# A routed expert stage: residual rows kept in sorted order instead of gathered by row number, and a single-tile ending

## What is computed

```python
logits = hidden @ router_w.T                      # 16 experts, the best one is taken (K = 1)
scores = sigmoid(top value)                       # 0 for the other 15 experts
routed_in = hidden * score
gate, up = split(routed_in @ gate_up_proj[e])     # 256 -> 2 x 256
routed_out = (up * silu(gate)) @ down_proj[e]     # 256 -> 256
shared = silu(hidden @ shared_gate_w.T) * (hidden @ shared_up_w.T) @ shared_down_w.T
x = layernorm(x + shared + routed_out)
```

## Time and profile before

| | |
|---|---|
| Median of three runs | 963.65 us |
| The profiled execution | 962.75 us |
| Its span, first to last instruction | 960.5 us |
| TensorE busy | 910.0 us, 95% |
| VectorE busy | 554.3 us, 58% |
| ScalarE busy | 351.4 us, 37% |
| GpSimd busy | 592.2 us, 62% |
| `route_and_share` begins | 680.5 us |
| `experts` begins | 844.1 us |

### The profile page before, as it was taken

The page is one execution under the profiler, slowest core; times in us unless marked ns, Lnnn a source line. Parts: engine busy times, 40 slices in busy tenths (PEclk is TensorE's granted clock), DMA queues, the critical chain, the costliest instruction groups (busy, mean ns, idle before and its releaser), DMA issues. The chain is left out here.

```text
span 960.5 us, 13006 instructions
## 1 busy us (share of the span) xinstructions
PE 910.0 (95%) x4616; PEld 537.4 (56%) x4616; DVE 554.3 (58%) x1123; ACT 351.4 (37%) x493; POOL 592.2 (62%) x397
## 2 busy tenths in 40 slices
PE   6998799999999999999999999999799999989993
PEld 2655354555565455555555465545578888855552
DVE  2897556667647667657667647644645121136562
ACT  2245244434335444425444425443341111124332
POOL 0453198888877888868888868893104400038885
PEclk9999899999999999999999999999799999999997
DMA  8013200000001000001000001040597100423310
GB/s 269 27 49 116 99 1 1 23 1 1 1 1 44 23 1 2 1 1 45 23 1 1 1 1 45 1 154 1 140 324 254 50 22 22 124 78 111 92 38 16
DMA packets 42873, 52.85 MB, mean 55 GB/s; under 512 B 4400, under 2 KB 33856, under 8 KB 42816
## 3 DMA queue, kind: packets, MB, share of 16 engines
q1 hardware_dynamic: 35808, 44.21, 14.7%
q0 software_dynamic: 3744, 6.32, 2.1%
q10 hardware_dynamic: 3264, 1.57, 0.6%
HBM read 38.42 MB, written 17.59 MB: 58 GB/s over the span
## 5 line engine op out<-in xcount | busy, mean ns | idle before, releaser
L600 POOL TENSOR_TENSOR accG<-accG,probs 128x1024 f32<-128x1024 f32 (+1 forms) x170 | 404.0, 2377 | 52.0 <-ACT probs L623 30.1
L623 ACT ACTIVATE probs<-st 128x1024 f32<-128x1024 f32 (+1 forms) x208 | 211.3, 1026 | 207.1 <-PE st L784 195.4
L667 DVE TENSOR_REDUCE mxp<-mx 128x1 f32<-128x512 f32 x360 | 231.6, 686 | 85.2 <-PE mx L770 79.0
L806 PE MATMUL av<-probs,V 128*64 128x512 f32 (+1 forms) x832 | 188.4, 596 | 0.0
L770 PE MATMUL mx<-K_hi,Q_hi 64*128 64x512 f32 (+1 forms) x480 | 164.0, 391 | 6.0 <-DVE mxp L667 4.5
L806 PEld LDWEIGHTS av<-probs,V 128*64 128x64 f32 (+1 forms) x832 | 56.8, 137 | 106.1 <-issue 100.6
L770 PEld LDWEIGHTS mx<-K_hi,Q_hi 64*128 64x128 f32 x480 | 78.9, 184 | 66.4 <-DVE mxp L667 34.5
L784 PE MATMUL st<-Q_hi,K_hi 64*128 64x512 f32 (+1 forms) x416 | 109.1, 440 | 0.9 <-ACT probs L623 0.9
L784 PE MATMUL st<-M,ones_r 64*128 64x512 f32 (+1 forms) x416 | 108.0, 394 | 0.0
L784 PE MATMUL st<-Q_hi,K_lo 64*128 64x512 f32 (+1 forms) x416 | 102.5, 391 | 0.0
L784 PE MATMUL st<-Q_lo,K_hi 64*128 64x512 f32 (+1 forms) x416 | 102.0, 390 | 0.0
(11 more groups left out here) (198 smaller groups left out, 1196.5 us busy)
## 6 DMA issues: line engine op xcount, KB each, us to landing
w_gate_up<-in_gate_up SPq DMA_DIRECT2D x4, 2048.0 KB, 20.8
w_down<-in_down SPq DMA_DIRECT2D x2, 2048.0 KB, 15.9
xs<-scratch_sorted_x SPq DMA_DIRECT2D x31, 128.5 KB, 2.1
scratch_sorted_x<-zero SPq DMA_DIRECT2D x7, 514.0 KB, 8.6
xT<-in_xT SPq DMA_DIRECT2D x4, 512.0 KB, 6.6
xring<-in_x SPq DMA_DIRECT2D x4, 512.0 KB, 9.4
scratch_x1b<-xT SPq DMA_DIRECT2D x4, 512.0 KB, 2.9
x<-scratch_x1b SPq DMA_DIRECT2D x4, 512.0 KB, 3.9
```

Source lines behind the costliest of these rows:

```text
L600: pool.tensor_tensor(total[0:r], so_far[0:r], probs[0:r, place(S, t)], ALU.add).then_inc(g_add, 1)
L623: act.activation(probs[0:r, place(S, t)], st[g % 2][0:r, :], ACT.Exp, scale=DH ** -0.5).then_inc(a_probs, 1)
L667: dve.tensor_reduce(mxp[:, F % 2, h * QT + i, j:j + 1], mx[h][:, 0:kn], AX.X, ALU.max).then_inc(v_mx, 1)
L806: mm = pe.matmul(av[h * DH:(h + 1) * DH, :], V[0:r, t, (2 * p + h) * DH:(2 * p + h + 1) * DH], probs[0:r, place(S, t), h * QC:(h + 1) * QC ...
```

## The change

- `routed` and its four `store_base` go. A new DRAM buffer `sorted_base` (31 tiles of 128 rows, 256 values) holds the base rows in sorted order. SP fills it with zeros from the tile `zero`, eight DMAs behind the last expert weight load of the gate and up part.
- In `route_and_share` POOL scatters `x2` tiles 0 to 11 into `sorted_base` by `pos`, 12 indirect DMAs behind its other 16, each after its tile's `v_base`, the first after the zero fill has landed (`d_bzero`).
- In `experts` POOL scatters tiles 12 to 15 first; the memory set of `base` and all 31 gathers go. SP waits for all 16 scatters, loads base tiles 0 to 3 with plain DMAs, and from then on takes turns: `xs` tile j, base tile j-4.
- The last three tiles (28, 29, 30, `SINGLE = 28`) have `inverse`, `shift` and the wait in `normalise` singly; POOL's stores stand between the inverses.

```diff
@@ route_and_share, sync
-            for c in range(CHUNKS - 1):
-                store_base(c)
+            for t in range(0, ETILES, ZT):
+                n = min(ZT, ETILES - t)
+                sp.dma_start(mem["sorted_base"].rearrange("(t p) n -> p t n", p=P)[:, t:t + n, :],
+                             zero[:, 0:D].unsqueeze(1).to_broadcast([P, n, D])
+                             ).then_inc(d_bzero, 16)
...
-            store_base(CHUNKS - 1)
@@ route_and_share, gpsimd
+            pool.wait_ge(d_bzero, 16 * ((ETILES + ZT - 1) // ZT))
+            for t in range(TILES - QT):
+                pool.wait_ge(v_base, t + 1)
+                pool.indirect_dma_start(mem["sorted_base"][:, :], bass.IndirectOffsetOnAxis(pos[:, t:t + 1], 0),
+                                        x2[:, t], None).then_inc(mem["d_base"], 16)
@@ experts, sync
             def load(j, r):
                 sp.wait_ge(p_x, j - UNROLL + 1)
                 sp.wait_ge(v_row, j - UNROLL + 1)
+                sp.sem_inc(filler, 1)
+                sp.dma_start(xs[:, r], xs_rows[:, bass.ds(j, 1), :].squeeze(1)).then_inc(d_xs[r], 16)
+            def load_base(j, r):
+                if not (isinstance(j, int) and j < AHEAD):
+                    sp.wait_ge(v_y, j - AHEAD + 1)
+                    sp.sem_inc(filler, 1)
+                sp.dma_start(base[:, r], base_rows[:, bass.ds(j, 1), :].squeeze(1)).then_inc(d_b[r], 16)
...
+            sp.wait_ge(mem["d_base"], 16 * TILES)
+            for j in range(AHEAD):
+                load_base(j, j)
+            for n in range(UNROLL):
+                turn(UNROLL + n, n)
@@ experts, gpsimd
-            pool.memset(base[:, :, :], 0.0).then_inc(g_c4, 1)
-            pool.wait_ge(g_c4, 3)
-            pool.wait_ge(mem["d_base"], 16 * CHUNKS)
-            def gather(j, r, reused):
...
+            for tile in range(TILES - QT, TILES):
+                pool.indirect_dma_start(mem["sorted_base"][:, :], bass.IndirectOffsetOnAxis(pos[:, tile:tile + 1], 0),
+                                        x2[:, tile], None).then_inc(mem["d_base"], 16)
...
-                if not (isinstance(j, int) and j + 2 >= ETILES):
-                    gather(j + 2, (n + 2) % UNROLL, not (isinstance(j, int) and j + 2 < AHEAD))
...
-            store(ETILES - 3, (ETILES - 3) % UNROLL)
-            store(ETILES - 2, (ETILES - 2) % UNROLL)
-            inverse(ETILES // 2, (ETILES - 1) % UNROLL, 1)
-            store(ETILES - 1, (ETILES - 1) % UNROLL)
+            inverse(single(SINGLE), SINGLE, SINGLE % UNROLL, 1)
+            store(SINGLE - 3, (SINGLE - 3) % UNROLL)
+            store(SINGLE - 2, (SINGLE - 2) % UNROLL)
+            inverse(single(SINGLE + 1), SINGLE + 1, (SINGLE + 1) % UNROLL, 1)
+            store(SINGLE - 1, (SINGLE - 1) % UNROLL)
+            store(SINGLE, SINGLE % UNROLL)
+            inverse(single(SINGLE + 2), SINGLE + 2, (SINGLE + 2) % UNROLL, 1)
+            store(SINGLE + 1, (SINGLE + 1) % UNROLL)
+            store(SINGLE + 2, (SINGLE + 2) % UNROLL)
@@ experts, vector
+                if isinstance(j, int) and j == SINGLE + 2:
+                    shift(single(SINGLE), SINGLE % UNROLL, 1)
+                elif n % 2 == 0 and not (isinstance(j, int) and (j < 3 or j > SINGLE + 2)):
                     shift(m - 1, (n - 2) % UNROLL, 2)
...
-            shift(ETILES // 2, (ETILES - 1) % UNROLL, 1)
+            shift(single(SINGLE + 1), (SINGLE + 1) % UNROLL, 1)
+            shift(single(SINGLE + 2), (SINGLE + 2) % UNROLL, 1)
```

More of the change, by code:

```diff
@@ L1315 @@
 AHEAD = 4
+SINGLE = ETILES - 3
 TURNS = (ETILES - 1) // UNROLL
@@ L1322, in experts @@
     w_gate_up, w_down = mem["w_gate_up"], mem["w_down"]
+    x2, pos = mem["x2"], mem["pos"]
     with ExitStack() as ctx:
@@ L1365, in _, with turn @@
             xs_rows = io["sorted_x"].rearrange("(t p) n -> p t n", p=P)
+            base_rows = mem["sorted_base"].rearrange("(t p) n -> p t n", p=P)
             def load(j, r):
[L1368 to L1376, removed]
                 sp.wait_ge(p_x, j - UNROLL + 1)
                 sp.wait_ge(v_row, j - UNROLL + 1)
-                load(j, j % UNROLL)
+                sp.sem_inc(filler, 1)
[5 more added lines that the diff above has]
+                sp.dma_start(base[:, r], base_rows[:, bass.ds(j, 1), :].squeeze(1)).then_inc(d_b[r], 16)
+            def turn(j, n):
+                if not (isinstance(j, int) and j >= ETILES):
+                    load(j, n)
+                if not (isinstance(j, int) and j - AHEAD >= ETILES):
+                    load_base(j - AHEAD, n % AHEAD)
+            sp.wait_ge(mem["d_base"], 16 * TILES)
[3 more added lines that the diff above has]
+                turn(UNROLL + n, n)
+            with sp.Fori(2, TURNS) as i:
+                for n in range(UNROLL):
+                    turn(i * UNROLL + n, n)
+            for j in range(TURNS * UNROLL, ETILES + AHEAD):
+                turn(j, j % UNROLL)
             for r in range(UNROLL):
@@ L1388, in _, with inverse @@
             pool.wait_ge(g_c4, 2)
-            pool.memset(base[:, :, :], 0.0).then_inc(g_c4, 1)
-            pool.wait_ge(g_c4, 3)
-            pool.wait_ge(mem["d_base"], 16 * CHUNKS)
-            def gather(j, r, reused):
[L1394 to L1406, removed]
+            for tile in range(TILES - QT, TILES):
+                pool.indirect_dma_start(mem["sorted_base"][:, :], bass.IndirectOffsetOnAxis(pos[:, tile:tile + 1], 0),
+                                        x2[:, tile], None).then_inc(mem["d_base"], 16)
+            def inverse(m, j, r, n):
+                tiles = slice(r - n + 1, r + 1)
+                pool.wait_ge(v_mv4, j + 1)
+                pool.tensor_tensor(ve4[:, tiles], mv4[:, tiles, 1], eps4[:, 0:n], ALU.add).then_inc(g_l4, 1)
                 pool.wait_ge(g_l4, m + 1)
-                pool.tensor_tensor(rstd4[:, pair], ve4[:, pair], mhalf4[:, 0:n], ALU.pow).then_inc(g_r4, 1)
+                pool.tensor_tensor(rstd4[:, tiles], ve4[:, tiles], mhalf4[:, 0:n], ALU.pow).then_inc(g_r4, 1)
             def store(j, r):
@@ L1449, in normalise @@
             def normalise(j, r, m):
-                if r % 2 == 0:
+                if m is not None:
                     act.wait_ge(v_shift, m + 1)
@@ L1470, in _ @@
                 slot(j, j % UNROLL, j // 2)
-            for j in range(ETILES - 4, ETILES):
-                normalise(j, j % UNROLL, j // 2)
+            normalise(SINGLE - 1, (SINGLE - 1) % UNROLL, None)
+            for j in range(SINGLE, ETILES):
+                normalise(j, j % UNROLL, single(j))
         @block.vector
```

17 lines of the change are left out of this document (7 added, 10 removed).

## The result

The changed kernel takes 956.25 us (median of six runs, 953.92 to 956.49), the kernel before 962.16 (six runs, 959.42 to 964.48). The ratio is 0.9935, 95% interval 0.9919 to 0.9952. So it became 5.9 us faster, where 3.0 were forecast with a median of 960.6 and a range from 957.0. The profiled execution has a span of 954.6 us against 960.5, a difference that a division by stage accounts for.

A forecast was written before the change was run, and what follows sets the result against it. TensorE was taken to bound the shared chunks, and POOL with gathers, a hair slower than TensorE, the expert tiles. Terms -0.5 + 0 + 0.3 - 0.8 - 2.0 = -3.0 us gave 960.6 us, range 957.0 to 964.5.

The forecast's parts named there:

- Where the sum started: Starting time: median of the runs before, 963.65 us, 0.9 above the profiled execution's 962.75, from which the terms were taken.
- The barrier: Between the blocks: without SP's last `store_base` the expert block starts 0.5 us sooner; bounds 0 and 0.6.
- The zero fill and twelve scatters: Shared part: issued beside 84 us in which TensorE never waits, they cost 0; bounds 0 and +1 us.
- The first base rows: Start of expert block: four scatters, landing and load make `whole(0)` late, holding `copy_h(1)`; 0.3 us lost.
- Rival 1: Start of expert block: shorter barrier keeps TensorE's clock up in the first `gate_up`, 1.9 us less, 958.7 us; chance 0.10.
- 1 and 3: Rival 3, block start: late base rows stall TensorE 1.4 us, a clock drop costs 3.1 more, 965.1 us; chance 0.10.
- The loop: Expert tiles: without gathers POOL no longer lags TensorE and `shift` finds the reciprocal ready; 0.8 us gained, bounds 0 and 1.1.
- The ending: Last three tiles: without gathers, with stores between single inverses, the last store starts sooner; 2.0 us gained, bounds 1.2 and 3.2.
- The last piece: From the last store to POOL's drain: stays at 6.4 us, so 0 gained.
- Rival 2: POOL's last drain: leftover work of 0.06 us per indirect DMA, 35 instead of 62 save 1.6 us, 959.0; chance 0.15.
- signs of being wrong: Wrong if TensorE idles after 850, shared chunks take over 84 us, or POOL's drain changes by over a microsecond.

The follow-up runs named there:

- e1: Changed kernel plus one DMA on SP's queue at the barrier between the blocks, writing the last shared tile's 128 rows to scratch; 956.25 us, ratio 0.9953.
- e11: The kernel of e8 again, on the chip where the changed kernel was also rerun; 954.52 us, ratio 0.9930.
- e9: Changed kernel plus a 512 KB store of four tiles of base rows to scratch on SP's queue at the barrier; 957.46 us, ratio 0.9959.
- e14: Kernel of e9 with POOL's base scatters held until the eight sums of the first two shared chunks are done; 955.02 us, ratio 0.9949.
- e12: The kernel before, unchanged, for a second profile; no median given, start and loop together 97.18 us.
- e5: Kernel before with only its ending changed: last three tiles singly, POOL's stores between the inverses; 960.11 us, ratio 0.9999.
- e4: Changed kernel plus 30 gathers into a spare tile on POOL, for which no other engine waits; 957.8 us, ratio 0.9973.
- e6: Changed kernel plus 26 gathers that nobody waits for, none in the ending; no median given, POOL's last drain ends 3.6 us behind SP's.
- e7: Changed kernel plus ten gathers that nobody waits for, in the first eight steps; no median given, POOL's last drain ends 2.3 us behind SP's.
- e8: Changed kernel with VectorE's base-row sum of tile 0 one slot later, and two stores and two normalisations moved earlier in the ending; 953.54 us, ratio 0.9933.
- e2: Changed kernel with base tiles 12, 13 and 14 scattered before the barrier, only tile 15 behind it; 955.85 us, ratio 0.9955.
- e13: Kernel of e8 with POOL's base scatters held until the eight sums of the first two shared chunks are done; 952.91 us, ratio 0.9927.
- e15: The kernel of e13 again, for a second profile; no median given, sums of the second shared chunk 3.45 us apart.

## Why the prediction was wrong

**Where the sum started** (963.65). The prediction took the median of the three runs known then. That of the six in the result is 962.16, so 1.5 us of the 4.35 between 960.6 and 956.25 come from this and have nothing to do with the change; the terms account for the other 2.9.

**The barrier** (-0.5) was right, in size and in cause: -0.52, and e1 brought 0.47 of it back with one DMA.

**The zero fill and twelve scatters** (0, at most +1): in the seven profiles on chip 13 fill and scatters cost TensorE nothing. They slowed the first scatters of scaled rows, which landed in 3.4 to 6.7 us there against 2.6 to 3.8 before, and these had the cover that was claimed for them. In the other profiles the two brought the pause, 0.8 us on TensorE in the profiled execution, inside the bound, but 1.4 in e11 and 3.7 in e9, outside it. What was missed is that "POOL is busy for 4.89 of 84 us" is not yet room: it says nothing of VectorE standing still, and no row before had VectorE's sums beside so long a row of POOL's DMAs.

**The first base rows** (+0.3). The chain was as described and even a little quicker: `whole(0)` came 9.13 us after the block's start against the 9.5 to 9.8 that I had worked out. Yet `down(1)` waited for 1.60, because TensorE was ready 2.1 us earlier, with `gate_up(0)` sooner and at full clock. With the clock down, as the prediction had it, `down(1)` waits for nothing (e14), so there the rows would have cost 0, the other end of its 0 to 0.3. Rival 1 priced the clock at 1.9 us more to gain without asking what is late next. It was the base rows: with the clock down the start is 12.36 us (e14), with it up 12.11 to 12.20. The two rivals about this stretch, 1 and 3, were not independent.

**The loop** (-0.8; measured -0.86). The number was right and the reason half of it. I took 1.1 us of excess as all that POOL costs, from an execution in which TensorE had lost 1.6 us at the start and so gave POOL a lead. With the clock up (e12) the excess is 2.6 us against the changed kernel's loop. Start and loop together are 97.1 and 97.2 us in the two profiles before, at either clock, and 95.7 to 95.95 after, with up to 1.6 of waiting for base rows in them. I read the row that POOL needs 6.29 us for two tiles against TensorE's 6.17 and did not draw the consequence that it suggests and that e5 and e12 bear out: what TensorE wins does not show while that holds. POOL's own load does make the excess of the first profile, since e4 brings it back with gathers that nobody waits for.

**The ending** (-2.0; measured -2.34), a little small and otherwise right: store after store it went as worked out, to a last store at 950.46 instead of 954.12. That POOL's freedom is the condition for it was not said.

**The last piece** (0; measured -2.24) is the term that failed, and its 2.24 us are most of the 2.9 that the terms missed. The time lies 0.75 us outside the range. Without this error it would have been 958.5, inside. The lower median of the runs before was enough for that too: without it the time would have been 957.7. "What lies between the last store and the end stays" was the failed step. Rival 2 had the mechanism, work left over in proportion to the indirect DMAs, at 0.06 us each and a chance of 0.15. It is 0.08 us each in this block, shown by e4, e6 and e7. The rows had shown that the drain ended 3.7 us after all data had landed, and a piece that long whose content is unknown deserved the larger chance. Two of the prediction's own signs of being wrong appeared: TensorE idled after 850, by 1.60 us, and POOL's drain behind SP's changed by over a microsecond.

With 2.2 us for the drain the sum would have been -5.2 us, which lies within the interval of the ratio (0.9919 to 0.9952 of 962.16, so 4.6 to 7.8 us).

## What to carry to other kernels

Where one engine's own work per round is as long as the critical engine's, look for the sum that does not move from one execution to the next before pricing any single wait: a better ending was worth nothing until POOL's gathers had gone. A faster clock at the start was worth nothing beside the gathers either, and at most 0.25 us beside the late base rows. Indirect DMAs on POOL cost twice here: 1.3 us each of its queue and, above 35 in the block, 0.08 us each at the last barrier. When a wait is taken away at a block's start, ask which chain of transfers is next in line; here it paid to let the engine ask for the data later (e8) and not to send the data sooner (e2). And when a cure is tried, try it on the chip that showed the illness: e13 to e15 did not, and so show nothing of the pause.

## What the runs showed of the hardware that was not expected

- POOL's drain ends later than the landing of its last data by an amount that grows with the count of indirect DMAs in the block: 1.3 us at 32, 1.5 at 35, 2.3 at 45, 3.6 at 61, 3.7 at 62, 4.0 at 65.
- In kernels that scatter base rows two of VectorE's sums stood 6 to 10 us apart instead of 3.45 in six of six profiles on chips 2 and 4 and in that of after, and in none of seven on chip 13. The cause is open.
- With a 512 KB store issued at a barrier, TensorE's first product behind it began 1.6 to 1.7 us after the block's first transpose in five profiles of five; with a 128 KB one in the same place (e1) or none it was 1.0 to 1.25.
- A scatter of 128 rows, which lands in 2.4 us, took 5.1 to 6.6 us beside a 2 MB load (e2), and 3.4 to 6.7 us at the time of the 4 MB zero fill (the profiles on chip 13).
